# Attention on one NeuronCore: the stream of row maxima starts four ticks earlier and is spread evenly, and additions on GpSimd wait only for earlier ones of the same heads

## The chip, the core and the metric

The program runs on one NeuronCore of a Trainium2 chip. Five engines share the work: TensorE (PE; its weight loads are listed as PEld), VectorE (DVE), ScalarE (ACT), GpSimd (POOL) and SyncE (SP), which only issues transfers here. Each engine takes its own instructions in the order in which they are written, and waits on semaphores that the others raise. The metric is the device time of one execution in microseconds (us). The kernel before takes 2926.89 us (median of 3 runs, 2926.59 to 2929.13).

## What is computed

One transformer block on x of shape 4 x 1024 x 1024 (batch, tokens, width), in float32: a layer norm with modulation, attention with 32 query heads on 8 key heads (4 query heads share one key head), a residual, and a second layer norm with a linear layer and LoRA. The change touches the attention alone:

```
h = _layernorm(x, axis=-1) * (1 + ca) + sa
q, k, v = h @ Wq, h @ Wk, h @ Wv          # heads of 32, q and k rotated by position
att = einsum('bhgqd,bhkd->bhgqk', qg, k) / sqrt(32)
att = where(causal, att, -inf)
probs = softmax(att, axis=-1)
ctx = einsum('bhgqk,bhkd->bhgqd', probs, v)
x = x + ga * (ctx @ Wo)
```

## The kernel before

Four stages follow one another: `modulation`, `qkv`, `attention`, `linear_half`. The change is in the tables that order `attention` and in one function of it.

**Groups and ticks.** Attention goes through 32 groups n (4 batches times 8 key heads; a group has 4 query heads, `G`, and 1024 tokens). The work of a group on the scores is cut into 20 units `EXP_UNITS` (key block j by query half `hf`, with two heads or all four). A tick u is one round of `group_steps(n)`: TensorE makes the transposed scores of unit u (step "scores", L876 and the causal mask L880) into one of two banks `scores`, ScalarE takes their exponential (L756) into `p_sum` (for j = 0) or a ring of 8 places `p_ring`. Two ticks later (`LAG`) TensorE multiplies them by V (step "values", L912, one per quad of units, into `ctx_ps`). This document writes S, V for these steps.

**Maxima.** The exponential needs the row maximum of each query before the group's scores are made: it enters as two more rows of the stacked operand. So while group n is worked on, TensorE also makes the scores of group n+1 the other way round, query by key (step "max", 38 units `MAX_UNITS`, L892, L894, with the mask L898), into three rotating banks `scores_q`, and VectorE reduces each to a row maximum (L800). A step "max" may not overwrite a bank before the reduction of three steps earlier has read it. "turn" and "sum" steps rotate through the same three banks. M0 to M37 are the 38 units below. After M37 VectorE runs `split_max`: it joins the two halves (L806, both inputs in SBUF), rounds to a high part (L811) and subtracts for the low part (L813, again two inputs in SBUF). The first reduction of the next group stands behind that on VectorE. TensorE then transposes the result (step "turn", L920, tick 17), ScalarE copies it (L775), and SyncE issues two transfers into the stacked operand (L697). The first scores of the next group wait for those.

**Where the maxima stand.** `max_ticks` puts two units in each of ticks 0 to 9 and three in each of ticks 10 to 15, and none in 16 to 19. All belong to group n+1.

**Denominators.** GpSimd adds the probabilities of 15 units per group into `p_sum` (function `add` under `@block.gpsimd`, L851), 4 for the first half of the queries and 11 for the second. The first addition of a half waits for the V step that still reads `p_sum` as probabilities. Every addition waits for the one before it, whatever it adds to. `sums` (L930, L935) multiplies `p_sum` by ones: the half 0 sum at tick 12, the half 1 sum at tick 6 of the next group, and for the last group after everything else.

## Time and profile before

| | |
|---|---|
| median of 3 runs | 2926.89 us |
| the profiled execution itself | 2926.28 us |
| its span, first to last instruction | 2924.5 us |
| PE busy | 2654.2 us (91%) |
| POOL busy | 1669.8 us (57%) |
| DVE busy | 1641.4 us (56%) |
| ACT busy | 1024.9 us (35%) |
| mean granted TensorE clock | 0.947 of full speed |

The profiled execution is one run; its own time is 1.8 us above its span and 0.6 us under the median. Shares are means over four stages with different limits. The attention stage runs from about 700 us to 2091 us. A busy PE is not PE at its peak, since the ends of matmuls are modelled; what TensorE does is read from the start of one step to the start of the next.

### The profile page before, as it was taken

What the parts mean: (1) busy time and instruction counts of PE and PEld (TensorE: products, weight loads), DVE (VectorE), ACT (ScalarE), POOL (GpSimd) and SP (SyncE); (2) the same over time, 40 slices, a digit from 0 to 9 for tenths busy, and PEclk for the clock granted to TensorE, in tenths of its full rate; (3) what the DMA queues carried; (4) which work ended last, traced back from release to release, by engine and by line L of the source; (5) the groups of instructions that cost most, each with busy time, mean ns of one, the idle gap of its engine ahead of it and who ended that gap; (6) DMA issues with size and microseconds to landing.
All of it is one profiled execution on the core that took longest, in us unless ns stands there. A gap on an engine that the chain in (4) does not pass through costs nothing. (4 is left out here: it accounts for less than half of the span.)

```text
span 2924.5 us, 37728 instructions
## 1 busy us (share of the span) xinstructions
PE 2654.2 (91%) x14588; PEld 1891.7 (65%) x14588; DVE 1641.4 (56%) x2483; ACT 1024.9 (35%) x1320; POOL 1669.8 (57%) x869
## 2 busy tenths in 40 slices
PE   2599999997999999999999999999559999999998
PEld 0378888885555555555555555555358878888887
DVE  2466666655566666665665666566134545455553
ACT  0333333321445545554554445444321111111111
POOL 0443333331577778777877877777515555455543
PEclk8799999997799999999999999999779999999999
DMA  9433333324222222222132212220252333333330
GB/s 347 143 128 113 115 112 109 112 80 126 63 66 58 70 67 54 70 70 67 45 80 70 67 40 70 70 61 18 77 173 80 94 109 95 100 108 94 108 97 34
DMA packets 178696, 267.55 MB, mean 91 GB/s; under 512 B 12197, under 2 KB 105509, under 8 KB 178393
## 3 DMA queue, kind: packets, MB, share of 16 engines
q1 hardware_dynamic: 178520, 265.13, 30.8%
q8 instruction: 120, 1.97, 0.3%
q14 instruction: 56, 0.45, 0.1%
HBM read 183.19 MB, written 80.84 MB: 90 GB/s over the span
## 5 line engine op out<-in xcount | busy, mean ns | idle before, releaser
L851 POOL TENSOR_TENSOR p_sum<-p_sum,p_ring 128x1024 f32<-128x1024 f32 (+2 forms) x480 | 1033.0, 2152 | 354.4 <-PE ctx_ps L912 284.3
L800 DVE TENSOR_REDUCE neg_max<-scores_q 128x1 f32<-128x512 f32 (+3 forms) x1216 | 729.8, 656 | 512.9 <-PE scores_q L894 327.3
L756 ACT ACTIVATE p_ring<-scores 128x1024 f32<-128x1024 f32 (+2 forms) x512 | 459.3, 917 | 405.4 <-PE scores L880 282.6
L894 PE MATMUL scores_q<-k_stack,q_stack 96*128 96x512 f32 (+3 forms) x1536 | 472.7, 387 | 4.1
L876 PE MATMUL scores<-q_stack,k_stack 98*128 98x512 f32 (+1 forms) x1216 | 438.8, 439 | 5.0 <-DMA q_stack<-neg_max_rows 4.9
L876 PEld LDWEIGHTS scores<-q_stack,k_stack 98*128 98x128 f32 x1216 | 197.4, 196 | 302.1 <-issue 172.2
L894 PEld LDWEIGHTS scores_q<-k_stack,q_stack 96*128 96x128 f32 x1536 | 281.1, 195 | 74.0 <-DVE neg_max L800 45.3
L579 PE MATMUL proj_ps<-h_hi,w_hi 128*128 128x512 f32 x768 | 304.8, 397 | 1.5 <-POOL h_lo L529 1.5
L579 PE MATMUL proj_ps<-h_hi,w_lo 128*128 128x512 f32 x768 | 300.3, 391 | 0.0
L579 PE MATMUL proj_ps<-h_lo,w_hi 128*128 128x512 f32 x768 | 300.1, 391 | 0.0
L536 POOL TENSOR_TENSOR roped_hilo<-roped_hilo 128x512 fp32r<-128x512 f32 x80 | 104.1, 1302 | 333.3 <-ACT roped_hilo L418 333.3
L912 PE MATMUL ctx_ps<-p_ring,v 128*32 128x512 f32 (+3 forms) x2560 | 280.7, 513 | 0.0
L1261 POOL TENSOR_TENSOR h_scaled<-h_scaled,mod_now 128x512 f32<-128x512 f32 x64 | 65.4, 1042 | 351.8 <-DVE h_scaled L1215 351.8
L1286 PE MATMUL po<-wo_hi,ctx_hi 128*128 128x512 f32 x512 | 204.1, 399 | 5.6 <-DVE wo_lo L1206 5.6
L1327 PE MATMUL pf<-we_hi,h_hi 128*128 128x512 f32 x512 | 200.4, 391 | 5.8 <-POOL h_lo L1265 5.8
L1286 PE MATMUL po<-wo_lo,ctx_hi 128*128 128x512 f32 x512 | 200.9, 392 | 0.0
L1286 PE MATMUL po<-wo_hi,ctx_lo 128*128 128x512 f32 x512 | 200.7, 392 | 0.0
L1327 PE MATMUL pf<-we_lo,h_hi 128*128 128x512 f32 x512 | 200.2, 391 | 0.0
L1327 PE MATMUL pf<-we_hi,h_lo 128*128 128x512 f32 x512 | 200.2, 391 | 0.0
L756 ACT ACTIVATE p_sum<-scores 128x1024 f32<-128x1024 f32 x128 | 131.0, 1024 | 142.3 <-PE scores L880 82.1
L898 PE MATMUL scores_q<-mask_q_k,ident_r 128*128 128x128 f32 x768 | 174.6, 227 | 0.0
L406 ACT COPY proj_raw<-proj_ps 128x512 f32<-128x512 f32 x96 | 56.2, 586 | 333.4 <-PE proj_ps L579 333.4
(130 smaller groups left out, 3844.9 us busy)
## 6 DMA issues: line engine op xcount, KB each, us to landing
q_stack<-qk_t SPq DMA_DIRECT2D x96, 512.0 KB, 6.9
qk_t<-roped_hilo SPq DMA_DIRECT2D x80, 512.0 KB, 2.8
wm<-in_L_wmod SPq DMA_DIRECT2D x12, 2048.0 KB, 19.9
x_in<-in_L_attn_resid SPq DMA_DIRECT2D x32, 512.0 KB, 6.4
ctx_t<-ctx_raw SPq DMA_DIRECT2D x64, 256.0 KB, 2.0
ctx_tile<-ctx_t SPq DMA_DIRECT2D x32, 512.0 KB, 4.0
inv_sums<-inv_t SPq DMA_DIRECT2D x128, 128.0 KB, 5.4
x_tile<-in_L_attn_resid SPq DMA_DIRECT2D x32, 512.0 KB, 3.3
```

The lines of the kernel that those rows point to most:

```text
L536: nc.gpsimd.tensor_tensor(lo, lo.bitcast(F32), qst[r % QST][:, 0, :].bitcast(F32), ALU.subtract).then_inc(s_rl.sem, 1)
L579: last = nc.tensor.matmul(pps[e % PPS][:, :], w[a][:, c, k, :], h[m % 2][i][:, k, :], start=(k == 0 and n == 0), stop=(k == DC - 1 and n = ...
L756: nc.scalar.activation(probs(n, u), src, ACT.Exp, scale=SM_SCALE).then_inc(s_ex.sem, 1)
L800: nc.vector.tensor_reduce(negm[:, lo // HALF, hs[0]:hs[-1] + 1, i:i + 1], src, AX.X, ALU.max, negate=True).then_inc(s_mx.sem, 1)
L851: nc.gpsimd.tensor_tensor(a, a, probs(n, u), ALU.add).then_inc(s_ap.sem, 1)
L876: last = nc.tensor.matmul(o[a], ks[0:KS, n % QS, j * P:(j + 1) * P], qs[0:KS, n % QS, h0:h0 + per, lo:lo + w], start=True, stop=not diag)
L894: last = nc.tensor.matmul(dst[:, a, :], qs[0:MHI, n % QS, h, i * P:(i + 1) * P], ks[0:MHI, n % QS, lo:lo + w], start=not first, stop=not d ...
L898: last = nc.tensor.matmul(dst[:, a, w - P:w], identr[:, :], maskS[:, 0, :], start=False, stop=True)
L912: last = nc.tensor.matmul(cps[DH * h:DH * (h + 1), lo - hf * HALF:HALF], V[:, b % 2, j, g * DH:(g + 1) * DH], p[:, a, :], start=(j == 0), ...
L1261: nc.gpsimd.tensor_tensor(v, v, cur[:, 4 * h:4 * h + 4, 1:2].broadcast_to([P, 4, P]), ALU.add).then_inc(s_hf.sem, 1)
L1286: last = nc.tensor.matmul(po[h][:, :], cs[slot][a][:, k, :], wo[w][:, k, h * HALF:(h + 1) * HALF], start=(k == 0 and n == 0), stop=(k == D ...
L1327: mm = nc.tensor.matmul(pf[h][:, :], hs[a][:, k, :], we[w][:, k, h * HALF:(h + 1) * HALF], start=(k == 0 and n == 0), stop=(k == DC - 1 an ...
```

## The change

The table of maxima is replaced by a formula, tick = m * 20 // 38 - 4. M0 to M7 of a group get a negative tick: they now run in ticks 16 to 19 of the group two before the one they belong to, that is directly ahead of the group before it. M8 to M37 stand in ticks 0 to 15, two a tick or one (one in ticks 5 and 15). M0 to M7 of group 1 stand between the first turn and the first scores. The count of instructions is the same on TensorE, VectorE, ScalarE and GpSimd; nothing is left out. On GpSimd each addition now waits only for the last earlier one of the same half that shares a head with it; `s_ap` still counts all of them.

```diff
+AHEAD = 4
 TURN_AT = 17
-def max_ticks():
-    ticks, left = [[] for _ in range(NE)], list(range(NM))
-    for t in range(NE):
-        for _ in range(2 if t < 10 else 3):
-            if left and t < TURN_AT:
-                ticks[t].append(left.pop(0))
-    assert not left
-    return ticks
-MAX_TICKS = max_ticks()
+MAX_TICK = [m * NE // NM - AHEAD for m in range(NM)]
...
-        if n + 1 < NG:
-            steps += [("max", n + 1, m) for m in MAX_TICKS[u]]
+        for at, t in ((n + 1, u), (n + 2, u - NE)):
+            if at < NG:
+                steps += [("max", at, m) for m in range(NM) if MAX_TICK[m] == t]
...
-STEPS = [("max", 0, m) for m in range(NM)] + [("turn", 0)] + [s for n in range(NG + 1) for s in group_steps(n)]
+STEPS = [("max", 0, m) for m in range(NM)] + [("turn", 0)] + [("max", 1, m) for m in range(NM) if MAX_TICK[m] < 0]
+STEPS += [s for n in range(NG + 1) for s in group_steps(n)]
...
             def add(n, u):
                 hf, j, hs, lo, w = EXP_UNITS[u]
-                place = NP * n + POOL_ADDS.index(u)
+                place = POOL_ADDS.index(u)
+                same = [p for p in range(place) if EXP_UNITS[POOL_ADDS[p]][0] == hf and set(EXP_UNITS[POOL_ADDS[p]][2]) & set(hs)]
...
-                if place:
-                    pool.wait_ge(s_ap.sem, s_ap.at(place))
+                if same:
+                    pool.wait_ge(s_ap.sem, s_ap.at(NP * n + same[-1] + 1))
```

TensorE of the kernel before, ticks 16 to 18 of group 0: the scores of two units, the turn (L920), a V step (L912), and the next scores.

```order
L876 MATMUL scores0<-q_stack,k_stack 128x384 [waits probs_ready]
L876 MATMUL scores0<-q_stack,k_stack 128x384
L880 MATMUL scores0<-mask_k_q,ident_r 128x128 x2
L876 MATMUL scores1<-q_stack,k_stack 128x384 [waits probs_ready]
L876 MATMUL scores1<-q_stack,k_stack 128x384
L880 MATMUL scores1<-mask_k_q,ident_r 128x128 x2
L920 MATMUL scores_q0<-consts,neg_max_hilo 128x128 [waits max_taken,max_lo]
L912 MATMUL ctx_ps<-p_ring,v 32x512 [waits probs_ready]
L912 MATMUL ctx_ps<-p_ring,v 32x512 x3
```

TensorE of the changed kernel at the same place, from the second unit's scores on (tick 17). L887 and L891 are the maxima's matmuls (L894, L898 before), L913 is the turn, L905 the V step; scores_q0, q1 and q2 are the three rotating banks.

```order
L869 MATMUL scores1<-q_stack,k_stack 128x384 [waits probs_ready]
L869 MATMUL scores1<-q_stack,k_stack 128x384
L873 MATMUL scores1<-mask_k_q,ident_r 128x128 x2
L887 MATMUL scores_q2<-k_stack,q_stack 128x256 [waits max_taken]
L891 MATMUL scores_q2<-mask_q_k,ident_r 128x128
L887 MATMUL scores_q2<-k_stack,q_stack 128x256
L891 MATMUL scores_q2<-mask_q_k,ident_r 128x128
L887 MATMUL scores_q0<-k_stack,q_stack 128x384 [waits max_taken]
L891 MATMUL scores_q0<-mask_q_k,ident_r 128x128
L913 MATMUL scores_q1<-consts,neg_max_hilo 128x128 [waits max_taken,max_lo]
L905 MATMUL ctx_ps<-p_ring,v 32x512 [waits probs_ready]
L905 MATMUL ctx_ps<-p_ring,v 32x512 x3
```

M2 and M3 of the group after next now stand between the scores of tick 17 and the turn (M0 and M1 stand in tick 16). M3 writes the bank that M0 used, so it waits for the reduction of M0, and that stands behind `split_max` on VectorE.

GpSimd of the kernel before, the additions of one group.

```order
L851 TENSOR_TENSOR p_sum<-p_sum,p_ring 128x2x384 [waits probs_added_pool,values_done,probs_ready] x2
L851 TENSOR_TENSOR p_sum<-p_sum,p_ring 128x4x256 [waits probs_added_pool,values_done,probs_ready]
L851 TENSOR_TENSOR p_sum<-p_sum,p_ring 128x4x128 [waits probs_added_pool,values_done,probs_ready]
L851 TENSOR_TENSOR p_sum<-p_sum,p_ring 128x1024 [waits probs_added_pool,values_done,probs_ready] x8
L851 TENSOR_TENSOR p_sum<-p_sum,p_ring 128x2x384 [waits probs_added_pool,values_done,probs_ready] x2
L851 TENSOR_TENSOR p_sum<-p_sum,p_ring 128x4x256 [waits probs_added_pool,values_done,probs_ready]
```

The same in the changed kernel (L844).

```order
L844 TENSOR_TENSOR p_sum<-p_sum,p_ring 128x2x384 [waits values_done,probs_ready] x2
L844 TENSOR_TENSOR p_sum<-p_sum,p_ring 128x4x256 [waits probs_added_pool,values_done,probs_ready]
L844 TENSOR_TENSOR p_sum<-p_sum,p_ring 128x4x128 [waits probs_added_pool,values_done,probs_ready]
L844 TENSOR_TENSOR p_sum<-p_sum,p_ring 128x1024 [waits values_done,probs_ready] x2
L844 TENSOR_TENSOR p_sum<-p_sum,p_ring 128x1024 [waits probs_added_pool,values_done,probs_ready] x6
L844 TENSOR_TENSOR p_sum<-p_sum,p_ring 128x2x384 [waits probs_added_pool,values_done,probs_ready] x2
L844 TENSOR_TENSOR p_sum<-p_sum,p_ring 128x4x256 [waits probs_added_pool,values_done,probs_ready]
```

The order is the same. Four additions of a group lose the wait altogether; the six wide ones and the two of 384 columns now wait for the addition before the last; three (units 4, 5 and 18) still wait for the one directly before them.

## Rows read from the trace of the kernel before

**Rows 1.** Waits over the whole span: engine, line, waited for: us, times, longest.
```profile
PEld scores_q L920 <- DVE neg_max_hilo L813: 76.0, 32, 2.4
POOL p_sum L851 <- POOL p_sum L851: 69.6, 411, 0.2
PEld scores_q L894 <- DVE neg_max L800: 45.3, 135, 0.5
```

**Rows 2.** Busy time by window; PEclk is the granted clock of TensorE.
```profile
1334.60:1370.00 35.40, 34.60 (x232) 21.66 (x232) 24.30 (x41) 18.81 (x22) 24.78 (x13) 1.00 0.29 69
1372.05:1375.46 3.41, 3.41 (x14) 1.56 (x14) 0.00 (x0) 0.27 (x1) 3.24 (x2) 0.50 0.04 10
```

**Rows 3.** Timeline, PE: start us, us, line, tiles [idle before]; four turns in succession.
```profile
1371.75 0.33 PE L920 MATMUL scores_q<-consts,neg_max_hilo 128*128 128x128 f32 x1 [2.25 <-DVE neg_max_hilo L813]
...
1413.98 0.33 PE L920 MATMUL scores_q<-consts,neg_max_hilo 128*128 128x128 f32 x1 [2.27 <-DVE neg_max_hilo L813]
...
1454.66 0.47 PE L920 MATMUL scores_q<-consts,neg_max_hilo 128*128 128x128 f32 x1 [2.23 <-DVE neg_max_hilo L813]
...
1498.05 0.33 PE L920 MATMUL scores_q<-consts,neg_max_hilo 128*128 128x128 f32 x1 [2.27 <-DVE neg_max_hilo L813]
```

**Rows 4.** Timeline of one group, from tick 10 to its turn.
```profile
1353.82 0.74 PE L876 MATMUL scores<-q_stack,k_stack 98*128 98x512 f32 x2
1354.06 2.39 POOL L851 TENSOR_TENSOR p_sum<-p_sum,p_ring 128x1024 f32<-128x1024 f32 x1 [3.50 <-PE ctx_ps L912]
...
1366.66 0.50 PE L894 MATMUL scores_q<-k_stack,q_stack 96*128 96x512 f32 x1
...
1367.15 1.06 PE L912 MATMUL ctx_ps<-p_ring,v 128*32 128x512 f32 x8
...
1368.43 0.74 DVE L806 TENSOR_TENSOR neg_max<-neg_max 128x16 f32<-128x16 f32 x1
...
1368.77 0.56 PE L876 MATMUL scores<-q_stack,k_stack 98*128 98x384 f32 x2
...
1369.31 2.34 POOL L851 TENSOR_TENSOR p_sum<-p_sum,p_ring 128x1024 f32<-128x1024 f32 x1 [0.17 <-POOL p_sum L851]
1369.42 2.27 DVE L813 TENSOR_TENSOR neg_max_hilo<-neg_max,neg_max_hilo 128x32 fp32r<-128x32 f32 x1
```

**Rows 5.** From the page's list of groups: the reductions on VectorE; busy us, mean ns.
```profile
L800 DVE TENSOR_REDUCE neg_max<-scores_q 128x1 f32<-128x512 f32 (+3 forms) x1216 | 729.8, 656 | 512.9 <-PE scores_q L894 327.3
```

**Rows 6.** Timeline, PE: M0 to M3 of a group and what follows.
```profile
1291.88 0.45 PE L892 MATMUL scores_q<-mask_q_k,ident_r 128*128 128x512 f32 x1
...
1293.11 0.64 PE L912 MATMUL ctx_ps<-p_ring,v 128*32 128x256 f32 x8
...
1294.41 0.33 PE L894 MATMUL scores_q<-k_stack,q_stack 96*128 96x256 f32 x1
...
1294.88 0.38 PE L894 MATMUL scores_q<-k_stack,q_stack 96*128 96x384 f32 x1
```

**Rows 7.** Timeline of the linear stage: VectorE and GpSimd without waits between additions.
```profile
2312.81 2.40 POOL L1240 TENSOR_TENSOR ctx_tile<-ctx_tile,inv_sums 128x1024 f32<-128x1024 f32 x1
2313.27 2.48 DVE L1169 TENSOR_TENSOR x_tile<-x_tile,gated 128x512 f32<-128x512 f32 x1
2315.16 2.85 POOL L1273 TENSOR_TENSOR x_tile<-x_tile,gbias 128x1024 f32<-128x1024 f32 x1
```

**Rows 8.** Timeline of the stage's start: split, turn, first scores, first maxima of group 1.
```profile
736.60 0.19 DVE L813 TENSOR_TENSOR neg_max_hilo<-neg_max,neg_max_hilo 128x32 fp32r<-128x32 f32 x1
736.84 0.48 PE L920 MATMUL scores_q<-consts,neg_max_hilo 128*128 128x128 f32 x1 [1.44 <-DVE neg_max_hilo L813]
740.51 1.22 PE L876 MATMUL scores<-q_stack,k_stack 98*128 98x512 f32 x2 [3.19 <-DMA q_stack<-neg_max_rows]
```

**Rows 9.** Timeline, end of the stage: first half 1 addition of group 30, last sum.
```profile
2027.76 2.39 POOL L851 TENSOR_TENSOR p_sum<-p_sum,p_ring 128x1024 f32<-128x1024 f32 x1 [3.50 <-PE ctx_ps L912]
...
2089.23 1.93 PE L930 MATMUL scores_q<-p_sum,ones_v 128*32 128x512 f32 x8 [13.74 <-POOL p_sum L851]
```

## The prediction

> **What bounds the kernel now.** I read the page first: TensorE is busy for 91% of the span, the others 57% or less, so the question is where TensorE stands still inside the attention stage (32 groups). The sum of waits comes next [rows 1]. Two entries stop TensorE in every group. The turn (L920) waits for the low part of the maxima (L813): 76.0 us over 32 groups, 2.4 us a group. The matmuls of the maxima (L894) wait for VectorE to free a bank: 45.3 us over 31 groups in the loop, 1.45 us a group. GpSimd waits for its own addition before: 69.6 us in 411 waits, 0.17 us each; that is no wait of TensorE.
>
> The timeline of the turns then gives the length of a group [rows 3]: 42.23, 40.68 and 43.39 us, three groups in 126.30 us, and this trio repeats. The mean is 42.10 us. The longer ones hold a stretch at half speed. Right after the turn at 1371.75 the granted clock is 0.50 for 3.4 us, which is 1.2 GHz, where the 35 us before the wait ran at 1.00, 2.4 GHz [rows 2]. In between TensorE had stood for 2.25 us at the turn [rows 3]. The groups with such a stretch are 1.55 and 2.71 us longer than the one without, on average 1.42 us. So a group of 42.10 us is 40.68 us at full speed, of which 2.4 and 1.45 are waits for VectorE; the bare TensorE work is 36.8 us.
>
> Last I read one group from tick 10 to its turn [rows 4], since the moved wait depends on who is where. L806 starts at 1368.43 and ends at 1369.17, L813 starts at 1369.42 and ends at 1371.69. The GpSimd addition beside it runs from 1369.31 to 1371.65. Both are tiny operations: without an addition beside it L813 took 0.19 us [rows 8]. Each has two inputs in SBUF and ends 0.03 to 0.05 us after a GpSimd addition ends. L806 waits for the rest of the running one, L813 comes 0.25 us later and waits for nearly all of the next. So the split of the maxima is set by the beat of GpSimd, 2.54 us from start to start (the seventh addition of the half starts at 1369.31, the first at 1354.06 [rows 4]). This agrees with the Trainium skill, page "SBUF — State Buffer", section "Who interferes with whom": a VectorE instruction with two SBUF inputs and a GpSimd one that reads SBUF take turns on a shared port, for a whole instruction each. The sum uses only the rows.
>
> **The maxima, ticks 10 to 15.** Before, 18 units stand there, now 11, and VectorE reduces one in 0.66 us [rows 5], so that three cost it 2 us a tick. Nearly all of the 1.45 us of bank waits lie there. With two units, 1.3 us, VectorE keeps up with a tick, which is 1.8 us of bare TensorE work on average (36.8 / 20). I keep 0.15 us of it. Gain 1.3 us a group.
>
> **The turn.** I follow one group in units of time after the start of tick 10's scores (1353.82 in rows 4).
> M37 starts at 12.84 before [rows 4]. Seven units (M20 to M26) leave the stretch. One with two heads and their masks takes 0.47 [rows 6]; I put two at that and the five of one head at 0.28, an estimate, together 2.3 us, and about 1.0 of bank waits with them: M37 starts at 9.5. Its matmuls take 0.4 and its reduction 0.7, so L806 is asked for at 10.7.
> GpSimd's first addition of the second half starts 0.24 after tick 10's scores, since it waits for a V step of TensorE [rows 4]. The wait of 3.50 us before it shows that it has slack. How fast the additions follow each other without the wait, no L851 row shows. In the linear stage two of the same size stand with 2.35 us between their starts [rows 7]; with the wait it is 2.54. I take 2.35, since it is the same operation on as many elements. Additions then end at 9.6, 12.0 and 14.3.
> L806 waits until 12.0, L813 until 14.35. The next reduction, M0 of the group after next, takes 0.7 and ends at 15.1.
> TensorE after M37's start: M37 0.4, V step and the scores of tick 16 1.62 (1367.15 to 1368.77 in rows 4), M0 and M1 1.13 (1.23 in rows 6, less 0.1 for the change over to a V step), scores of tick 17 0.57, M2 0.47 [rows 6]: 4.2. It reaches M3 at 13.7 and must wait for M0's reduction: 1.4 us. The turn behind it needs the bank of M1, reduced 0.6 later: another 0.3. So 1.7 us of waits stand where 2.4 stood: gain 0.7 a group. The wait isn't taken away but moves from the turn to M3; and the earlier end of M37 is worth little, because the split ends on a beat of GpSimd.
> Bounds: if L806 falls just ahead of an addition's end, the whole is one beat of 2.35 shorter and no wait is left (gain 2.4); if it falls just behind one, it is one beat longer.
> The six maxima M2 to M7 behind tick 17's scores also give the stack transfers cover. From turn to first scores the shortest that I see is 3.67 us [rows 8], partly that transfer; now 4.8 us of TensorE work lie there. No new wait.
>
> **The clock.** The half-speed stretches follow a wait of 2.25 us. A wait of 1.4, then 0.3 after M3's matmuls, leaves TensorE with more to do. I take the stretches as gone: gain 1.42 us a group. The bound from the other side is that they stay: 0.
>
> **GpSimd alone.** Ten of fifteen additions start 0.2 us sooner, 2 us a group. It has slack in the loop, so this is worth nothing by itself, except that it brings the split's end from 15.5 to 14.35, which is in the sum above. At the end it is on the path: the last sum waits 13.74 us for the last addition, after an unbroken row of 26 additions from 2027.76 [rows 9]. Some 22 steps of 0.2 are 4.4 us; I keep 4. Here a rule of the Trainium skill speaks against me: "Perfetto Trace Analysis", section "GPSIMD Engine Instruction", has it that reported spans of GpSimd aren't reliable, and only the spacing of starts is. I use spacings only, but from another line. Were the spacing unchanged, the turn's gain would be nil and the tail's too.
>
> **The start.** M0 to M7 of group 1 now stand between the first turn and the first scores. Before, TensorE stood there for 3.19 us [rows 8]. The eight take about 3 us at full speed [rows 6], and the clock is at half there, so some 6 us: 2.5 us later than before. In the last groups the eight fewer units save nothing, as GpSimd sets the end.
>
> **The sum.** A group: 40.68 - 2.4 - 1.3 + 1.7 = 38.7 us against 42.10, 3.4 us less. Thirty groups lie between the first scores and the last row of additions: 102 us. With 2.5 lost at the start and 4 won at the end: 103.5. The profiled execution took 2926.3 us: 2822.8, and the median is 0.6 above it: about 2823.
>
> **Rivals.**
> 1. The half-speed stretches stay, since TensorE still stands for 1.7 us in each group. In the rows a 2.25 us wait brings one in two groups of three, so a shorter one may still do so in some. In all of them as before: 30 x 1.42 = 43 us back, 2866.
> 2. GpSimd's spacing stays at 2.54. The split ends at 15.5, the waits of TensorE are 2.6 and 0.3, the clock falls as before. Left are 1.3 us of bank waits less 0.5 of longer wait: 0.8 a group, 24 us, 2902. For it: no row of L851 without the wait. Against: all rows of the linear stage look like rows 7.
> 3. The other side: L806 misses the beat. I have it asked for at 10.7 and the addition ends at 12.0 (the one before at 9.6). If it is asked for after 12.0, because M37 is 1.3 us later than I think, the split and the waits are one beat longer: 4.0 us instead of 1.7 in each group. A group is 41.0 us at full speed, and with a wait that long I'd expect the longer of the half-speed stretches in each, 2.7: 43.7, 1.6 more than now, 30 groups, 2975. It decides at a delay of 1.3 us.
> 4. Without gaps between additions VectorE doesn't get in at all until GpSimd has a wait of its own, ten us later: far slower, beyond 3050. Against it: in rows 7 the second GpSimd operation follows the first with no gap, and L1169, asked for in the middle of the first, still ends 0.5 us after its end.
> 5. TensorE waits less than I say (L806 falls well, or the bank waits go altogether): down to 2.0 us a group less, 2765.
>
> **How the numbers follow.** My forecast 0.50 (its own range 2805 to 2845), rival 1, whole or in part, 0.22, rival 2 0.09, rival 3 0.05, rival 4 0.02, rival 5 0.09, and 0.03 for a change of under 0.2% by parts that cancel. 0.2% (5.9 us) is about what a measurement of this kernel can tell from no change. Faster 0.90, same 0.03, slower 0.07. The range 2785 to 2885 holds the forecast, rival 1 and a part of rivals 2 and 5.
>
> **What would show it.** In the profile after: turns 38.7 us apart and evenly; the wait of the turn for L813 gone from the list, and in its place the maxima's weight loads waiting for L800 once a group for 1.4 us, behind L813; L806 about 1.2 us long and L813 still 2.3; additions 2.35 us apart; 1.00 as the granted clock in the loop; the last sum waiting for GpSimd. I'm wrong if L813 is short, if the turn still waits for it, or if groups come in trios of different length.

## The result and the profile after

The changed kernel takes 3196.66 us (median of 4 runs, 3180.24 to 3205.81) where the kernel before takes 2926.74 beside it: a ratio of 1.092 (95% interval 1.087 to 1.096). It was forecast at 2823 and is 270 us slower than before. The profiled execution took 3193.42 us, its span is 3191.6.

In the page's list of groups the reductions are as before (658 ns against 656 [rows 5]), but the join of the maxima (L798 now, L806 before) stands at 11 us each, where it took 0.74 before [rows 4]. Columns: busy us, mean ns.

```profile
L792 DVE TENSOR_REDUCE neg_max<-scores_q 128x1 f32<-128x512 f32 (+3 forms) x1216 | 745.1, 658 | 501.2 <-PE scores_q L891 332.1
L798 DVE TENSOR_TENSOR neg_max<-neg_max 128x16 f32<-128x16 f32 x32 | 355.6, 11114 | 1.1
```

The sum of waits (engine, line, waited for: us, times, longest) answers to [rows 1]. The turn's wait for the low part has gone in every group but the last, and GpSimd's waits for itself are down to 10.7 us. In their place the maxima's matmuls wait for a bank, 10 us at a time, and GpSimd waits for an exponential, 7 us at a time.

```profile
PEld scores_q L887 <- DVE neg_max L792: 305.8, 72, 10.1
PE scores_q L887 <- DVE neg_max L792: 288.5, 30, 10.0
POOL p_sum L844 <- ACT p_ring L748: 221.0, 32, 7.4
```

The timeline of one group, from the second addition of GpSimd's row on, shows the place: GpSimd, then VectorE, then TensorE. Columns as in [rows 3].

```profile
1325.36 19.85 POOL L844 TENSOR_TENSOR p_sum<-p_sum,p_ring 128x1024 f32<-128x1024 f32 x9
...
1331.67 2.07 DVE L792 TENSOR_REDUCE neg_max<-scores_q 128x1 f32<-128x512 f32 x3 [1.22 <-PE scores_q L891]
1333.77 11.47 DVE L798 TENSOR_TENSOR neg_max<-neg_max 128x16 f32<-128x16 f32 x1
1345.27 0.18 DVE L803 CAST neg_max_hilo<-neg_max 128x32 fp32r<-128x32 f32 x1
1345.49 0.19 DVE L805 TENSOR_TENSOR neg_max_hilo<-neg_max,neg_max_hilo 128x32 fp32r<-128x32 f32 x1
...
1346.53 0.69 PE L887 MATMUL scores_q<-k_stack,q_stack 96*128 96x384 f32 x1 [9.60 <-DVE neg_max L792]
...
1347.22 0.45 PE L913 MATMUL scores_q<-consts,neg_max_hilo 128*128 128x128 f32 x1
```

The join is asked for at 1333.77. GpSimd's row runs without a gap until 1325.36 + 19.85 = 1345.21, and the join ends at 1345.24. Five boundaries between additions pass in the meantime, and VectorE gets in at none. The row is ten additions long, and the program sets that length: the addition behind it (unit 18) still waits for the one directly before it. The same row, with the gap of 0.17 us behind it, stands in e9_reductions below, where TensorE never stands still:

```profile
1321.21 22.34 POOL L853 TENSOR_TENSOR p_sum<-p_sum,p_ring 128x1024 f32<-128x1024 f32 x10 [3.10 <-PE ctx_ps L914]
1343.73 2.39 POOL L853 TENSOR_TENSOR p_sum<-p_sum,p_ring 128x1024 f32<-128x1024 f32 x1 [0.17 <-POOL p_sum L853]
```

In the changed kernel GpSimd then stands for 7.04 us and not 0.17, because the exponential of unit 18 isn't there: its scores stand behind the turn on TensorE, and TensorE stands at M3 for 9.60 us, since M3's bank is freed by a reduction behind the join. The cast and the subtraction fall into that time and take 0.18 and 0.19.

The windows of the same group (columns as in [rows 2]) show the price in clock.

```profile
1296.00:1331.00 35.00, 35.00 (x216) 20.42 (x214) 19.91 (x33) 17.57 (x21) 17.62 (x9) 0.88 0.30 73
1331.50:1345.50 14.00, 5.43 (x39) 4.06 (x37) 13.64 (x6) 3.46 (x4) 13.71 (x7) 0.76 0.00 1
1347.00:1352.00 5.00, 5.00 (x20) 2.77 (x20) 1.56 (x4) 1.12 (x2) 0.00 (x0) 0.50 0.03 7
```

After the stand the clock is at 0.50 (1.2 GHz). The first window begins just behind the turn before, so it holds such a stretch too, and its 35 us average 0.88. The next join starts at 1384.97, so this group has 51.2 us. From the second turn to the last, over 30 groups, the mean is 50.9 us, against 42.1 before: 263 us of the 267 by which the span is longer.

### The profile page after: what moved, and what is told of

It reads as the page before. It is cut to its first block and busy times, and to the rows that moved or that the text cites. A ratio compares the mean times of both kernels' runs of the same rounds, so it can differ in the third digit from the quotient of the medians.

```text
span 3191.6 us, 37728 instructions
## 1 busy us (share of the span) xinstructions
PE 2709.0 (85%) x14588; PEld 1941.4 (61%) x14588; DVE 1926.3 (60%) x2483; ACT 1030.2 (32%) x1320; POOL 1654.8 (52%) x869
## 5 line engine op out<-in xcount | busy, mean ns | idle before, releaser
L844 POOL TENSOR_TENSOR p_sum<-p_sum,p_ring 128x1024 f32<-128x1024 f32 (+2 forms) x480 | 1018.3, 2152 | 641.0 <-PE ctx_ps L905 409.2
L792 DVE TENSOR_REDUCE neg_max<-scores_q 128x1 f32<-128x512 f32 (+3 forms) x1216 | 745.1, 658 | 501.2 <-PE scores_q L891 332.1
L887 PE MATMUL scores_q<-k_stack,q_stack 96*128 96x512 f32 (+3 forms) x1536 | 506.8, 404 | 288.5 <-DVE neg_max L792 288.5
L887 PEld LDWEIGHTS scores_q<-k_stack,q_stack 96*128 96x128 f32 x1536 | 302.0, 208 | 337.1 <-DVE neg_max L792 305.8
L869 PE MATMUL scores<-q_stack,k_stack 98*128 98x512 f32 (+1 forms) x1216 | 452.5, 450 | 0.1
L869 PEld LDWEIGHTS scores<-q_stack,k_stack 98*128 98x128 f32 x1216 | 205.2, 204 | 318.7 <-ACT p_ring L748 154.5
L798 DVE TENSOR_TENSOR neg_max<-neg_max 128x16 f32<-128x16 f32 x32 | 355.6, 11114 | 1.1
L905 PE MATMUL ctx_ps<-p_ring,v 128*32 128x512 f32 (+3 forms) x2560 | 302.8, 549 | 0.0
L891 PE MATMUL scores_q<-mask_q_k,ident_r 128*128 128x128 f32 x768 | 187.6, 244 | 0.0
```

The costliest lines, as they stand in the source:

```text
L792: nc.vector.tensor_reduce(negm[:, lo // HALF, hs[0]:hs[-1] + 1, i:i + 1], src, AX.X, ALU.max, negate=True).then_inc(s_mx.sem, 1)
L798: nc.vector.tensor_tensor(both[0], both[0], both[1], ALU.min).then_inc(s_mc.sem, 1)
L844: nc.gpsimd.tensor_tensor(a, a, probs(n, u), ALU.add).then_inc(s_ap.sem, 1)
L869: last = nc.tensor.matmul(o[a], ks[0:KS, n % QS, j * P:(j + 1) * P], qs[0:KS, n % QS, h0:h0 + per, lo:lo + w], start=True, stop=not diag)
L887: last = nc.tensor.matmul(dst[:, a, :], qs[0:MHI, n % QS, h, i * P:(i + 1) * P], ks[0:MHI, n % QS, lo:lo + w], start=not first, stop=not d ...
L891: last = nc.tensor.matmul(dst[:, a, w - P:w], identr[:, :], maskS[:, 0, :], start=False, stop=True)
```

## The experiments

All are compared with the kernel before on the same chip, which took 2923.7 to 2926.8 us (medians) beside e1 to f3 and 2922.7 and 2929.8 beside f4 to f6. Where an interval stands, the kernel was timed four times; the others are one run each. "Row" means GpSimd's gapless additions of the second half of the queries, and "asked for" is the start of the VectorE instruction.

**Each half of the change alone.** e1_max_only takes the new table and leaves GpSimd's wait as it was; e2_pool_only is the kernel before with the new wait.

```diff
 e1_max_only (from the changed kernel)
-                if same:
-                    pool.wait_ge(s_ap.sem, s_ap.at(NP * n + same[-1] + 1))
+                if place:                      # place = NP * n + POOL_ADDS.index(u)
+                    pool.wait_ge(s_ap.sem, s_ap.at(place))
```

> The new places of the maxima with the old waits of GpSimd (every addition waits for the one before it). Theory A, the port: VectorE's join of the maxima (two inputs in SBUF) gets in only in a gap between two additions, and the old wait of 0.17 us is such a gap. Then the join takes at most one addition (under 2.6 us) and not 11.5, the low part one more (2.3 us), TensorE waits at M3 for 1.5 to 3 us, the bank waits of ticks 10 to 15 are gone: 2880 to 2925 us. Theory B, the order: M3 ahead of the turn waits for a reduction that stands behind the split, and this alone costs the 270 us, whatever GpSimd does: 3100 us or more.

Measured: 2942.77 us, ratio 1.006 (1.005 to 1.008), 18 above its range. No join is held off.

```profile
L805 DVE TENSOR_TENSOR neg_max_hilo<-neg_max,neg_max_hilo 128x32 fp32r<-128x32 f32 x32 | 71.2, 2224 | 1.1
L798 DVE TENSOR_TENSOR neg_max<-neg_max 128x16 f32<-128x16 f32 x32 | 57.3, 1790 | 1.1
```

M3 waits, and this time the stretch at half speed comes in every group, not in two of three as before [rows 3]:

```profile
1335.48 0.69 PE L886 MATMUL scores_q<-k_stack,q_stack 96*128 96x384 f32 x1 [2.07 <-DVE neg_max L792]
...
1336.50:1340.00 3.50, 3.50 (x14) 1.61 (x14) 0.58 (x2) 0.27 (x1) 3.16 (x3) 0.50 0.04 9
1341.00:1375.00 34.00, 34.00 (x231) 20.95 (x231) 22.60 (x37) 19.25 (x23) 24.35 (x13) 0.98 0.31 75
```

From turn to turn a group has 42.5 or 42.9 us, alternately. What the maxima's new places win is spent on a wait of 2.07 us at M3 and on the clock behind it.

> The old places of the maxima with the new waits of GpSimd. Theory A: the join (L806) is asked for while additions follow each other without a gap and gets in when GpSimd next stands, after the addition of unit 17, some 7 us later; then the low part takes 0.19 us. The turn comes about 4 us later than before, the half-speed stretches grow: 3040 to 3120 us. Theory B: nothing but the end of the stage changes: 2920 to 2927 us.

Measured: 3099.61 us, 1.061 (1.059 to 1.063). GpSimd's waits alone, in the old order, hold the join off (7.6 us on average, the loop's 7.87), and the turn waits instead of M3. The join is asked for in the row's seventh addition and gets in behind the tenth; the low part then takes 0.19. A group has 47.8 us.

```profile
L806 DVE TENSOR_TENSOR neg_max<-neg_max 128x16 f32<-128x16 f32 x32 | 244.2, 7630 | 1.1
```

**Is it the join's size?** e3_wide_join widens the tile so that the join works on 512 elements a partition (496 more than it needs; their values are constants).

```diff
-        negm = sb("neg_max", [P, 2, G, TT])
+        negm = sb("neg_max", [P, 2, G, 128])
...
-                both = [negm[:, s, :, WIDE[0]:] for s in range(2)]
+                both = [negm[:, s, :, :] for s in range(2)]
```

> The changed kernel with a join of 512 elements in place of 16 (the tile of maxima is widened to 128 columns a head, of which 8 carry data; the other elements are constants). In the other stages VectorE instructions of 512 elements with two SBUF inputs get in between two GpSimd instructions without a gap. If size is what tells them from the join, this join ends 0.5 us after the end of the running addition (1 to 3 us in all), and the low part of 32 elements starves in its place, for about 9 us: time about as the changed kernel's, 3150 to 3220. If size is not it, the join itself still takes about 11.5 us, and the low part 0.2: 3180 to 3220.

Measured: 3182.67 us, and the join 11.6 us on average. The size is not it.

```profile
L800 DVE TENSOR_TENSOR neg_max<-neg_max 128x512 f32<-128x512 f32 x32 | 372.1, 11629 | 1.1
```

**Gaps only where the split stands.** e4_four_gaps keeps the own wait at units 13 to 16.

```diff
-                if same:
+                if u in (13, 14, 15, 16):
+                    pool.wait_ge(s_ap.sem, s_ap.at(NP * n + place))
+                elif same:
                     pool.wait_ge(s_ap.sem, s_ap.at(NP * n + same[-1] + 1))
```

> The changed kernel in which the additions of units 13 to 16 again wait for the one directly before them (the four that stand where the split is asked for). Theory A: the join takes under 2.5 us, the low part 2.3, and what was forecast for the change comes: groups of 38 to 40 us, 2815 to 2880 us. Theory B: no change against the changed kernel, 3190.

Measured: 2887.54 us, 0.988 (0.986 to 0.990), 8 above its range: four gaps of 0.17 us a group give back 309 us. The join is asked for where it was in the changed kernel, in the fifth addition of the row, but now a gap follows that addition, and the join gets in there: 1.0 us in all 31 groups of the loop. So this is the kernel that comes nearest to what the prediction described, with four gaps left in. TensorE at three turns, the first with its M3, and the window behind the first turn:

```profile
1310.15 0.45 PE L889 MATMUL scores_q<-k_stack,q_stack 96*128 96x384 f32 x1 [1.27 <-DVE neg_max L792]
1310.84 0.30 PE L915 MATMUL scores_q<-consts,neg_max_hilo 128*128 128x128 f32 x1 [0.18 <-DVE neg_max L792]
1351.45 0.30 PE L915 MATMUL scores_q<-consts,neg_max_hilo 128*128 128x128 f32 x1 [0.18 <-DVE neg_max L792]
1393.89 0.45 PE L915 MATMUL scores_q<-consts,neg_max_hilo 128*128 128x128 f32 x1
...
1311.20:1314.60 3.40, 3.40 (x15) 1.71 (x10) 0.55 (x2) 0.43 (x2) 3.06 (x3) 0.52 0.04 10
```

The waits are 1.27 at M3 and 0.18 at the turn (forecast: 1.4 and 0.3), and the shortest groups have 39.0 us (forecast: 38.7). But most have 40.5 or 42.0, with a mean of 40.9, because the half-speed stretch is still there behind most turns.

**The split without two SBUF inputs.** If VectorE's two-input instructions are what is held off, a split made of instructions with one input should not care. e5_one_input makes the join, the difference and the negation by `tensor_reduce` over a strided view and keeps the rounding as a plain copy. e6_one_input_old_order has that split in the kernel before, e7_one_input_max_only has it in e1.

```diff
+                pairs = joined[:, :, :].rearrange("p s m -> p m s")
-                nc.vector.tensor_tensor(both[0], both[0], both[1], ALU.min)
+                nc.vector.tensor_reduce(joined[:, 0:1, :]..., negm[...].rearrange("p s h i -> p (h i) s"), AX.X, ALU.min)
...
-                nc.vector.tensor_copy(mhl[:, 0:G * TT], flat)
+                nc.vector.tensor_copy(mhl[:, 0:G * TT], joined[:, 0, :])
...
-                nc.vector.tensor_tensor(mhl[:, G * TT:2 * G * TT], flat, mhl[:, 0:G * TT].bitcast(F32), ALU.subtract)
+                nc.vector.tensor_reduce(joined[:, 1:2, :]..., mhl[:, 0:G * TT]..., AX.X, ALU.add, negate=True)
+                nc.vector.tensor_reduce(mhl[:, G * TT:2 * G * TT]..., pairs, AX.X, ALU.add)
```

> The changed kernel with a split of the maxima that reads one SBUF operand per instruction: the join as a reduction by minimum over the two halves, the low part as a reduction by sum over the pair (joined, minus high part); one small instruction more. The values are the same. Theory A, the port: none of them waits for GpSimd, the split takes 0.8 us in place of 12, TensorE waits neither at M3 nor at the turn, the clock stays at full speed in the loop: groups of 36.8 to 37.5 us, 2760 to 2800 us. If anything but the two SBUF inputs held the split up (the tiny size, the place behind gapless additions as such), it stays near 3190.

Measured: 3201.41 us, 1.093 (1.091 to 1.096): missed by 400 us. The three reductions pass beside GpSimd's row, but the plain copy does not:

```profile
L805 DVE CAST neg_max_hilo<-joined 128x32 fp32r<-128x32 f32 x32 | 347.5, 10859 | 1.1
L800 DVE TENSOR_REDUCE joined<-neg_max 128x32 f32<-128x64 f32 x32 | 7.1, 222 | 1.1
L812 DVE TENSOR_REDUCE neg_max_hilo<-joined 128x32 fp32r<-128x64 f32 x32 | 7.0, 220 | 1.1
L807 DVE TENSOR_REDUCE joined<-neg_max_hilo 128x32 f32<-128x32 f32 x32 | 5.9, 186 | 1.1
```

So two inputs aren't the criterion. A copy from SBUF to SBUF is held off as well, and takes the join's place in the row. The Trainium skill, page "SBUF — State Buffer", section "Who interferes with whom", lists copy and cast among the instructions that can take the shared port and says that `tensor_reduce` never does on trn2. Both agree with these four rows (10.9 us against 0.2).

> The kernel before (old order, old waits of GpSimd) with the same one-operand split. The turn no longer waits 2.4 us a group, and the half-speed stretches behind that wait go: 42.1 - 2.2 - 1.4 = 38.5 us a group, 2810 to 2830 us. The bank waits of ticks 10 to 15 stay, 1.45 us a group. If the half-speed stretches come from something else: 2850 to 2860.

Measured: 2832.25 us, 0.968 (0.966 to 0.969), 2 above its range. With gaps in the row, a split with one instruction that can be held off instead of three is worth 94 us. TensorE still waits for banks (45.3 us in all, as in [rows 1]), 0.2 us at most turns, and the clock is 1.00 in the loop.

> The new order of the maxima, the old waits of GpSimd, the one-operand split. Against the one with the new waits too this tells what those are worth once the split doesn't care: in the loop nothing as long as GpSimd has slack (36.1 us of additions and gaps in a group of 37), at the end of the stage 4 us. 2765 to 2805 us, 3 to 10 above its partner.

Measured: 2795.99 us, 0.956 (0.954 to 0.958). e1 with this split: 147 us less, so it was the split's beats, and the clock behind them, that ate the gain of the new places.

**The copy gone too.** In e9_reductions (new waits) and e10_reductions_max_only (old waits) the high part is a reduction over one element as well.

```diff
-                nc.vector.tensor_copy(mhl[:, 0:G * TT], joined[:, 0, :])
+                nc.vector.tensor_reduce(mhl[:, 0:G * TT]..., joined[:, 0:1, :]..., AX.X, ALU.add)
```

> The changed kernel with a split made of reductions alone: join by minimum, high part as a reduction over one element, minus high part, low part by sum. In the run before, the one plain copy of the split (SBUF to SBUF, 128 x 32) took 11.2 us where it stood behind gapless additions; the reductions took 0.2. Theory A (the copy needs the shared port as the two-input instructions do, reductions don't): the split takes 0.9 us, TensorE waits at neither place, the clock stays up in the loop: 2760 to 2795 us. Rival: the second instruction of any split starves, whatever it is: 3190.

Measured: 2774.02 us (2773.22 to 2775.62), 0.949 (0.947 to 0.950), the fastest of all. The split takes 0.9 us in a row of additions without a gap, and TensorE stands nowhere in the loop:

```profile
1331.97 0.22 DVE L800 TENSOR_REDUCE joined<-neg_max 128x32 f32<-128x64 f32 x1
1332.22 0.18 DVE L806 TENSOR_REDUCE neg_max_hilo<-joined 128x32 fp32r<-128x32 f32 x1
1332.44 0.19 DVE L809 TENSOR_REDUCE joined<-neg_max_hilo 128x32 f32<-128x32 f32 x1
1332.66 0.22 DVE L814 TENSOR_REDUCE neg_max_hilo<-joined 128x32 fp32r<-128x64 f32 x1
...
1290.00:1410.00 120.00, 120.00 (x826) 75.40 (x828) 77.93 (x138) 68.39 (x81) 104.51 (x50) 1.00 0.27 65
```

Every group of the loop but the last has 37.18 us, at a granted clock of 1.00 (2.4 GHz).

> The same split of reductions, the new order of the maxima, the old waits of GpSimd. With the copy in it (1.55 us there) this was 2796 us; 1.3 us less in the split matters only as far as TensorE still waited for it: 2775 to 2796. Against the run with the new waits it prices those waits: I expect it 3 to 8 us above.

Measured: 2778.47 us, 0.950 (0.948 to 0.952), also 37.18 us a group. The new waits, once nothing depends on the gaps, are worth 4.5 us by the medians (the two sets of times just touch), and none of it in the loop.

**Form or place?** The kernel before has gapless GpSimd instructions in its linear stage, and VectorE gets in there [rows 7]. Three kernels put one more VectorE instruction beside the row, on SBUF of its own: f1_spare_add an addition of 512 elements behind M28 (tick 10), f2_spare_late the same directly ahead of the join, f3_spare_min_early a minimum of 4x4 scattered elements, the join's form, behind M28.

```diff
 f1_spare_add
                     take_max(n, step[2])
+                    if step[2] == 28:          # f2: NM - 1
...
+                        nc.vector.tensor_tensor(spare[:, 0, :], spare[:, 0, :], spare[:, 1, :], ALU.add)...
```

> The changed kernel with one more VectorE instruction a group, behind the reduction of M28 (tick 10), where additions follow each other without a gap: an addition of 512 contiguous columns of spare tiles, both inputs in SBUF, in the form of those that get in between two GpSimd instructions in the linear stage. If the form of the VectorE instruction tells them from the join (minimum, 16 scattered elements), it ends 0.5 us after the running addition (under 3 us), and the time is that of the changed kernel within 30 us. If it is the row of additions that doesn't let it in, it takes 5 us or more, until TensorE, held up by missing reductions, leaves GpSimd without work, and the time rises by over 100 us.

> The spare addition of 512 contiguous columns that got in at tick 10 within 1.2 us, now behind the reduction of M37, just ahead of the join, where the fifth addition of a gapless row is running. Theory P (place: VectorE gets in early in a row of gapless additions, not late): it takes over 10 us here, and the join behind it 0.2. Theory F (form: an addition of 512 contiguous columns gets in, a minimum or a copy doesn't): it takes about 1.5 us, and the join behind it starves for some 10 us. Time near 3185 either way.

> At tick 10, where the spare addition got in, an instruction of the join's form instead: minimum of 4 x 4 scattered elements of spare tiles, both inputs in SBUF. Theory P: it gets in at the end of the running addition, under 1 us. Theory F: it starves there, 5 us or more.

Measured: f1 3179.74 us, the addition 1.22 us on average, the join still 11.5. f2 3206.01 us, the same addition 11.7. f3 3152.19 us, the minimum 0.72 us, the join at its late place 11.47. First f1, then f2:

```profile
L801 DVE TENSOR_TENSOR neg_max<-neg_max 128x16 f32<-128x16 f32 x32 | 368.8, 11526 | 1.1
L827 DVE TENSOR_TENSOR spare<-spare 128x512 f32<-128x512 f32 x32 | 38.9, 1216 | 0.0
```
```profile
L827 DVE TENSOR_TENSOR spare<-spare 128x512 f32<-128x512 f32 x32 | 375.4, 11731 | 0.0
L801 DVE TENSOR_TENSOR neg_max<-neg_max 128x16 f32<-128x16 f32 x32 | 5.2, 161 | 0.0
```

The same instruction gets in at the first boundary when it is asked for early in the row, and waits out the whole row when asked for in the fifth addition. In this row the place decides, not the form.

**Which place?** f4_gap_before_12 puts one gap back, ahead of the fifth addition, during which the join is asked for. f5_four_spares has the small minimum behind M28, M30, M32 and M34, one in each of the first four additions. f6_spare_by_group has a single one, in the second, third or fourth addition in three of four groups.

```diff
 f4_gap_before_12
-                if same:
+                if u == 12:
+                    pool.wait_ge(s_ap.sem, s_ap.at(NP * n + place))
+                elif same:
```
```diff
 f5_four_spares (f6: step[2] == (36, 30, 32, 34)[n % 4] and n % 4)
+                    if step[2] in (28, 30, 32, 34):
...
+                        nc.vector.tensor_tensor(few[0], few[0], few[1], ALU.min)...
```

> The changed kernel, but the addition of unit 12 waits again for GpSimd's own addition of unit 11, so that the row of gapless additions ends and starts anew just ahead of the addition during which the join is asked; the additions of units 13 to 17 still follow without a gap. Theory R (what holds VectorE off is how many gapless additions have gone before): the join gets in at the end of the addition of unit 12 or 13, 1 to 3.5 us instead of 11.5, its last subtraction within 2.5 us, the wait at M3 some 2 us instead of 10, and the kernel takes 2850 to 2920 us. Theory S (what counts is only what follows, a next addition that has long been ready; or the place in the tick order itself): the join waits 11 us again until GpSimd stops, and the kernel takes 3180 to 3210 us.

Measured: 2994.61 us. Theory R's join: asked for in the first addition of the restarted row, it gets in at its end. Its total was too low by 75 us, because the cast, asked for 0.04 us behind the join, and the subtraction each take one addition more, and TensorE waits 3.6 us at M3 in 29 of 30 groups.

```profile
1438.27 1.24 DVE L798 TENSOR_TENSOR neg_max<-neg_max 128x16 f32<-128x16 f32 x1
1439.55 2.31 DVE L803 CAST neg_max_hilo<-neg_max 128x32 fp32r<-128x32 f32 x1
1441.89 2.27 DVE L805 TENSOR_TENSOR neg_max_hilo<-neg_max,neg_max_hilo 128x32 fp32r<-128x32 f32 x1
```

> The changed kernel with four additional VectorE minima of 4x4 elements a partition in SBUF of their own, one each behind the reductions of M28, M30, M32 and M34 (ticks 10 to 13 of 20), where GpSimd is in its second to fourth addition of the gapless row; nothing waits for them but VectorE itself. Theory R: the first gets in at the first boundary (0.7 us, as measured), and one of the next three is the first that is held off, for 12 to 20 us until GpSimd stops; the reductions behind it then wait too and TensorE with them, and the kernel takes over 3200 us. Theory T (it is the join's tick alone, or what other engines do there, and the row has no part in it): all four take under 2.5 us and the join 11.5 as before, 3150 to 3180 us.

Measured: 2981.33 us; neither theory. All 124 minima of the loop get in at the next boundary, and all 31 joins behind them too, in an unbroken row of ten additions. Four useless instructions a group make the kernel 215 us faster than the changed one.

```profile
1428.70 0.72 DVE L829 TENSOR_TENSOR spare<-spare 128x16 f32<-128x16 f32 x1
1430.41 1.35 DVE L829 TENSOR_TENSOR spare<-spare 128x16 f32<-128x16 f32 x1
1432.88 1.21 DVE L829 TENSOR_TENSOR spare<-spare 128x16 f32<-128x16 f32 x1
1435.21 1.22 DVE L829 TENSOR_TENSOR spare<-spare 128x16 f32<-128x16 f32 x1
1438.26 0.50 DVE L801 TENSOR_TENSOR neg_max<-neg_max 128x16 f32<-128x16 f32 x1
...
1427.00 22.20 POOL L852 TENSOR_TENSOR p_sum<-p_sum,p_ring 128x1024 f32<-128x1024 f32 x10 [3.13 <-PE ctx_ps L913]
```

> The changed kernel with one additional VectorE minimum of 4x4 elements a partition in SBUF of its own in three of four groups, behind the reduction of M30 (asked during the second addition of the gapless row), M32 (third) or M34 (fourth), and none in the fourth. Theory R (the gapless boundaries that VectorE has let pass since the row began or since it last got in decide, four of them and three being too many so far, none being few enough): there is one number of passed boundaries, one to three, from which on spare minima and joins are both held off until GpSimd stops; a join asked in the fifth addition gets in at once after a minimum that got in one or two boundaries before, and in the groups without one it waits 11.5 us. Theory T (something at the join's tick, which four minima in a row happened to shift): the joins of all four kinds of group take 11 us, and the single minima 1.3 us. Theory U (the time since VectorE last used that port with two inputs, some microseconds, rather than boundaries): as R, and the minima in the second addition get in although none went before, since the row's first boundary was nobody's either. The kernel takes 3000 to 3180 us by R, 3150 to 3180 by T.

Measured: 3183.24 us. Three kinds of group in succession:

```profile
1376.33 1.87 DVE L829 TENSOR_TENSOR spare<-spare 128x16 f32<-128x16 f32 x1
1384.36 11.31 DVE L801 TENSOR_TENSOR neg_max<-neg_max 128x16 f32<-128x16 f32 x1
...
1429.74 1.89 DVE L829 TENSOR_TENSOR spare<-spare 128x16 f32<-128x16 f32 x1
1435.28 11.47 DVE L801 TENSOR_TENSOR neg_max<-neg_max 128x16 f32<-128x16 f32 x1
...
1483.06 13.08 DVE L829 TENSOR_TENSOR spare<-spare 128x16 f32<-128x16 f32 x1
1497.97 0.17 DVE L801 TENSOR_TENSOR neg_max<-neg_max 128x16 f32<-128x16 f32 x1
```

Over all groups of the loop the single minimum gets in at the next boundary in 8 of 8 cases in the second addition, in 7 of 8 in the third and in none of 8 in the fourth. The join, in the fifth, does not get in in any of the 22 groups in which it is asked for beside the row, also in the 15 where a minimum had got in, with only one or two boundaries let pass since. So it is neither a count of boundaries since VectorE last had its turn (theory R) nor the time since then (theory U). Theory T had the joins right, but it isn't the join's tick: the minimum of the fourth addition is held off at an earlier one, and in f5 the join gets in. What fits GpSimd's additions in e4 and in f1 to f6: in the first three of a gapless row VectorE gets in; from the fourth on it does so only if it got in at the boundary directly before, or where a gap follows (e4). In the linear stage even this doesn't hold, as the next section shows.

## Why the prediction was wrong

**The step that failed** is "L806 waits until 12.0, L813 until 14.35". It took for granted that VectorE gets in at the next boundary between two additions. In the kernel before that was always so, because every pair of additions had a gap of 0.17 us between them, and the change takes out those gaps. The change makes one row of ten additions, and the join waited for its end: 11.47 us instead of 1.3. It was asked for about where forecast, 11.0 us after tick 10's scores (10.7 forecast). The sign that was named for being wrong, a short L813, is there: 0.19. Rival 4 described this outcome, with its mechanism and its time ("ten us later", "beyond 3050"), and got 0.02. I set it aside on [rows 7], where VectorE does get in at a gapless boundary. That row is right, and it isn't even an early place in its row. The timeline of before, just ahead of it:

```profile
2308.31 2.04 POOL L1261 TENSOR_TENSOR h_scaled<-h_scaled,mod_now 128x512 f32<-128x512 f32 x2 [10.64 <-DVE h_scaled L1215]
2310.32 2.54 POOL L1265 TENSOR_TENSOR h_lo<-h_scaled,h_hi 128x512 fp32r<-128x512 f32 x2
...
2312.54 0.69 DVE L1167 TENSOR_TENSOR gated<-po,ga 128x512 f32<-128x512 f32 x1 [3.71 <-PE po L1286]
```

L1240 is the fifth instruction of this gapless row, and L1169, asked for in it, gets in at its end; the same happens in all 26 such places of the kernel before. L1167 ahead of it is not an earlier turn: it reads `po` from PSUM, and it takes 0.68 or 0.69 us all 64 times, beside GpSimd and without it. What the row doesn't bound is the price in another row: f1 and f2 show the same instruction getting in at one place of the row of L851 (L844 after) and not at another. Among those additions there was no gapless row before, so no row of mine came from the place in question, and rival 4 should have stood in the range with far more than 0.02. Why the fifth instruction is no obstacle in the linear stage and is one here stays open.

**GpSimd's own spacing** was right: additions 2.34 us apart in the loop (22.19 us for ten, two of them 1.8), forecast 2.35. "It has slack in the loop, so this is worth nothing by itself" was wrong in sign. The 0.17 us gaps were the opening through which VectorE got in. e2 shows what closing them costs alone (176 us against before), e4 what four of them are worth (309 us).

**Maxima and M3.** The bank waits of ticks 10 to 15 went for the most part. Of 305.8 us in which weight loads waited for a bank, the 30 waits at M3 are 293, which leaves 0.4 us a group (I had kept 0.15, out of 1.45). The wait moved from the turn to M3, as forecast, but at 9.60 us instead of 1.4. In e4, where the join gets in, it is 1.27 and 0.18 for a forecast of 1.4 and 0.3.

**The clock.** The prediction took the half-speed stretches as gone at waits of 1.4 and 0.3 us. In e4 they stay behind most turns (0.52 right after a turn), with a wait of 1.27. Rival 1, at 2866, would have been nearer than the forecast even if the join had got in: e4 took 2888. In the loops of e7, where the longest stand of a group is 0.19 us, and of e9 and e10, where there is none, the clock is 1.00.

**The sum as it stands.** A group of e9 has 37.18 us, without a wait and at full speed (the prediction's bare work: 36.8). M3's wait adds 9.60. The window of 35 us from the turn on, half-speed stretch included, runs at 0.88, which costs an estimated 12% of 35 or 4.2 us. Together 51.0, measured 51.2.

**Start and end.** From the first turn to the first scores there are now 5.9 us (735.47 to 741.40), 2.3 more than the 3.67 of [rows 8]; I had 2.5. The scores start only 0.9 later than before because the turn itself came 1.4 earlier in this execution. For the tail's gain, which I put at 4 us, the pair e10 and e9 is the cleanest: 4.5 by the medians, and from the last turn to the last sum 52.2 and 46.9 us in the two traces.

**The two halves.** e1 shows that the new places alone don't bring the forecast either (+0.6%): with the gaps left in, M3 waits 2.07 us, and the clock falls in every group. This is near to rival 2, which I had at 2902 with waits of 2.6 and 0.3 and the clock "as before". The waits were somewhat shorter (2.07, and 0.2 or none), and the clock was worse.

## What to carry to other kernels

Before taking a wait from an engine that shares something with another, ask who gets in through the gap. A gap of 0.17 us looked like loss in 411 places and was what let a 0.2 us instruction through. Where a tiny VectorE instruction on the critical chain stands beside a dense row on GpSimd, make it a form that isn't held off (here four `tensor_reduce` of 0.2 us) rather than trust the beat; here that brought 5.1% against the kernel before together with the new places, and 3.2% in the old order with one copy left in. And one row that shows a thing happening once doesn't bound its price at another place: weigh the rival by how bad it would be, and look for a row from that very place.

## What the runs showed of the hardware

- VectorE `tensor_tensor` with both inputs in SBUF, and also a plain SBUF-to-SBUF copy from fp32 to fp32r of 32 elements a partition, were held off for up to 13 us beside gapless GpSimd additions. `tensor_reduce` from SBUF, of 32 or 64 elements, took 0.19 to 0.22 us at the same place.
- Whether VectorE gets in at a gapless boundary depends on what went before. Beside additions of 2.34 us it did in the first three, and later only in unbroken succession or at a gap (one exception in f5, a cast that waited 10.42 us, and one in f6, a minimum in the third). In the linear stage a VectorE addition with both inputs in SBUF (L1169 before) got in at the end of the fifth instruction of a gapless row, 25 or 26 times in each of these kernels, and at the end of the sixth 3 times in each, without a turn before it in that row. So the number of instructions doesn't decide. The first four there last 1.04 to 1.29 us, so it may be a time since the row's start (in at 6.9 us there and at 7.1 behind the loop's third addition, not in at 9.4 behind its fourth); but the three entries at the sixth came at 9.2 to 9.3 us, which leaves little room for that. What in GpSimd brings the state about wasn't found.
- A 512-element addition that got in at f1's first boundary lengthened GpSimd's next addition from 2.38 to 2.84 us; the 4x4 minimum didn't measurably (2.38).
- The Trainium skill, page "SBUF — State Buffer", section "Who interferes with whom", has the two engines taking turns on a shared port for a whole instruction each, the second to issue blocked until the first finishes. In f5, where VectorE gets in at seven boundaries in succession, the trace agrees; the join of the changed kernel, which five boundaries pass by, waits for more than the one running instruction.
